# Moving a head's probability scaling one slot later, and its transposes behind the up product

## The reference

```
x  = hidden (8, 512, 512);  xn = layernorm(x)
attention: 16 query heads of 32, ONE key and one value head shared by all,
           rotary positions with a decay, causal mask, softmax over 512 keys,
           projection 512 -> 512 plus bias
shared:    relu(xn @ up.T)**2 @ down.T            (512 -> 1024 -> 512)
routed:    8 of 32 experts a token (2 of 4 groups), 256 -> 256 -> 256 in a latent
out = x + attention(xn) + shared(xn) + routed(xn)
```

## Time and profile before

| what | value |
|---|---|
| median of 3 runs | 1751.81 us (1751.12 to 1755.2) |
| the profiled execution | 1752.61 us, span 1750.6 us |
| PE busy | 1625.1 us, 93% of the span |
| DVE busy | 1201.7 us, 69% |
| ACT busy | 1072.9 us, 61% |
| mean granted clock of TensorE | 0.978 |

### The profile page before, as it was taken

How to read it: one execution, slowest core, us unless ns; L and a number is a source line. 1 busy time by engine, 2 the same in 40 slices (tenths; PEclk the granted TensorE clock), 3 DMA queues, 4 the chain that set the end, 5 groups by cost and what they waited for, 6 DMA issues and landing times.

```text
span 1750.6 us, 40616 instructions
## 1 busy us (share of the span) xinstructions
PE 1625.1 (93%) x10811; PEld 1390.9 (79%) x10811; DVE 1201.7 (69%) x3666; ACT 1072.9 (61%) x2799; POOL 821.5 (47%) x669
## 2 busy tenths in 40 slices
PE   5875779999999999999999999899999999999999
PEld 5765567787777777877777778689999999999987
DVE  6868877877777868777778687355555555555567
ACT  3344455775666757756757577366666666666652
POOL 0212001452444525424434254177777877777760
PEclk9897889999999999999999999999999999999999
DMA  7951722443434434334344344489999999988894
GB/s 280 380 163 43 145 64 84 150 123 119 145 111 149 141 106 143 127 117 152 115 147 137 96 147 134 124 168 192 177 196 189 190 182 203 202 173 158 141 257 184
DMA packets 193090, 273.71 MB, mean 156 GB/s; under 512 B 37400, under 2 KB 133791, under 8 KB 190820
## 3 DMA queue, kind: packets, MB, share of 16 engines
q0 software_dynamic: 60352, 92.59, 24.5%
q1 hardware_dynamic: 77572, 113.01, 22.8%
q10 hardware_dynamic: 54944, 65.52, 12.6%
HBM read 121.83 MB, written 129.67 MB: 144 GB/s over the span
## 4 chain that ended last, share of the span: by engine, by line
PE 63%; DVE 17%; issue 8%; DMA 5%; ACT 4%; POOL 2%; DVEq 1%; SPq 0%; ACTq 0%; POOLq 0%
PE e_psH L1701 12%; PE e_psY L1712 12%; DVE m_sc L1084 5%; PE m_psO L1330 4%; PE m_psU L64 3%; PE m_psT L1308 3%; PE m_psS L1283 3%; PE e_psX L1686 3%; PE m_psU L66 3%; PE m_psU L65 3%; PE m_psY L64 3%; PE m_psY L66 3%; PE m_psY L65 3%; DVE m_sc L1094 3%; ACT m_sc L930 2%
## 5 line engine op out<-in xcount | busy, mean ns | idle before, releaser
L1666 POOL DMA_INDIRECT sums<-e_y,e_where x287 | 446.0, 1554 | 155.0 <-issue 89.3
L852 POOL DMA_INDIRECT slot_rows<-m_row,slots x256 | 266.6, 1041 | 479.9 <-ACT m_sc L930 448.2
L930 ACT ACTIVATE m_sc<-m_sc,m_low 128x512 f32<-128x512 f32 (+3 forms) x512 | 283.8, 556 | 182.1 <-DVE m_low L1084 180.5
L1701 PE MATMUL e_psH<-e_xt,e_w_of 128*128 128x128 f32 x2296 | 303.6, 275 | 3.3 <-ACT e_xt L1561 3.3
L1712 PE MATMUL e_psY<-e_w,e_ht 128*128 x1148 | 295.8, 380 | 2.1 <-ACT e_ht L1572 1.9
L1084 DVE CUSTOM_DVE_ANT_0 m_sc<-m_psS,cst 128x512 f32<-128x512 f32 (+3 forms) x512 | 229.6, 485 | 88.2 <-PE m_psS L1283 85.6
L1701 PEld LDWEIGHTS e_psH<-e_xt,e_w_of 128*128 128x128 f32 x2296 | 279.1, 192 | 3.6 <-ACT e_xt L1561 3.5
L1567 ACT ACTIVATE e_w_of<-e_w 128x512 f32 x287 | 180.9, 630 | 121.4 <-issue 117.1
L1283 PE MATMUL m_psS<-m_ks,m_qs 96*128 96x256 f32 (+2 forms) x512 | 161.4, 375 | 74.1 <-DVE m_low L1084 67.1
L1712 PEld LDWEIGHTS e_psY<-e_w,e_ht 128*128 128x128 f32 x1148 | 196.4, 191 | 17.6 <-issue 3.0
L1622 DVE TENSOR_SCALAR e_where<-e_row,e_shifts 128x1 uint32<-128x1 uint32 x287 | 61.3, 214 | 197.2 <-DMA sums<-e_y,e_where 177.5
(11 more groups left out here) (229 smaller groups left out, 3235.3 us busy)
## 6 DMA issues: line engine op xcount, KB each, us to landing
e_row<-slot_rows ACTq DMA_DIRECT2D x287, 144.5 KB
m_qs<-m_qhi SPq DMA_DIRECT2D x256, 64.0 KB, 2.0
e_w<-in_w SPq DMA_DIRECT2D x256, 64.0 KB
f_xt<-in_x SPq DMA_DIRECT2D x8, 1024.0 KB, 11.0
m_qs<-m_qlo SPq DMA_DIRECT2D x128, 64.0 KB, 2.0
m_res<-in_x SPq DMA_DIRECT2D x8, 1024.0 KB, 6.2
sums<-empty POOLq DMA_DIRECT2D x32, 256.0 KB
partial<-m_res ACTq DMA_DIRECT2D x16, 512.0 KB
```

The source lines that it names most:

```text
L852: pool.indirect_dma_start(out=xs, out_offset=bass.IndirectOffsetOnAxis(ap=slots_sb[:, g, k:k + 1], axis=0), in_=row[g % 2][:, :], in_offse ...
L930: nc.scalar.activation(cols, cols, ACT.Exp, bias=low[:, h % 2, i:i + 1], scale=-1.0, accum_out=total[:, h % 2, i:i + 1]).then_inc(exp_done, 1)
L1666: pool.indirect_dma_start(out=both_sums, out_offset=bass.IndirectOffsetOnAxis(ap=where[u % NY][:, 0:1], axis=0), in_=y[u % NY][:, :], in_o ...
L1701: mm = pe.matmul(psH[u % 2][:, k * P:(k + 1) * P], w1_of[u % 2][:, c * INTER + k * P:c * INTER + (k + 1) * P], xt[u % 2][:, c * P:(c + 1) ...
```

## The change

`scale(s)` on DVE moves from the end of slot s to slot s + 1, between the first and the second pair of masks there; `shared` moves behind the second pair. On PE the first group of transposes moves from ahead of the values and the up product to behind them, so that the three groups stand together but for the queries' product. On ACT relu and square move ahead of the copy of the first group. Nothing is added or left out.

```
@@ act_program
+                    if s < NH:
+                        shared(s)
                     if 0 <= t < NH:
                         ta(t, 0)
-                    if s < NH:
-                        shared(s)
@@ dve_program
                         mask_and_min(s, ROWS[0])
                         mask_and_min(s, ROWS[1])
                     if 1 <= s <= NH:
+                        scale(s - 1)
+                    if s < NH:
+                        mask_and_min(s, ROWS[2])
+                        mask_and_min(s, ROWS[3])
+                    if 1 <= s <= NH:
                         shared(s - 1)
                     if s - 1 in Q_AT:
                         rotate(b, f"q{Q_AT[s - 1]}", (0,))
-                    if s < NH:
-                        mask_and_min(s, ROWS[2])
-                        mask_and_min(s, ROWS[3])
...
-                    if s < NH:
-                        scale(s)
                     if s - 2 in Q_AT:
                         low_part(b, f"q{Q_AT[s - 2]}")
@@ pe_program
                         scores(s, ROWS[2])
                         scores(s, ROWS[3])
-                    if 0 <= t < NH:
-                        transposes(t, 0)
                     if s > HC and s % HC == 1:
                         values(s // HC - 1, (0, 1, 3, 2))
                     if s < NH:
                         up(s)
                     if 0 <= t < NH:
+                        transposes(t, 0)
                         transposes(t, 1)
                     if s in Q_AT:
                         queries(b, Q_AT[s])
                     if 0 <= t < NH:
                         transposes(t, 2)
```

## The result

| | before | after |
|---|---|---|
| median | 1751.69 us (1751.12 to 1755.2, 4 runs) | 1783.39 us (1779.05 to 1784.9, 4 runs) |
| ratio | | 1.0161, 95% interval 1.0139 to 1.0183 |
| profiled execution, span | 1752.61, 1750.6 us | 1782.89, 1780.8 us |
| mean granted clock | 0.978 | 0.974 |

The changed kernel is slower by 1.6%. The prediction said 1778 us, range 1748 to 1798.

A forecast was written before the change was run, and what follows sets the result against it. PE was taken as busiest, above all in attention, waiting 18.3 us for VectorE's masks. Profiled 1752.6 + 23.8 (seven batches at +3.4) - 1.5 (first batch) + 4 (clock) = 1779, so 1778 us; range 1748 to 1798.

The forecast's parts named there:

- The wait before the reciprocal: VectorE idle until ScalarE's last exponential of a head, 76 times, 0.75 us each; the change was to remove it.
- slot 8: Slot with a query product, 8.73 us because VectorE comes late; VectorE would have caught up, so -0.74 us, near 8.0.
- slot 12: Plain slot losing its small wait for masks: 4.77 us becomes 4.57.
- Two small terms: Slot 4, query product after the relu: +0.10 us on 7.89; slot 15, a plain slot, shortened like slot 12.
- Transposes behind up: Slots 5, 9, 13: third transpose group waits for ScalarE's copy of the first; +0.77, +0.77, +0.60 us a batch.
- Rotation behind the squares: Slots 2, 6, 10: VectorE idle 0.7 us during ScalarE's rounding, next mask late; +0.70, +0.80, +0.80 us a batch.
- First batch: Six waits before the reciprocal saved, -5.0 us; transposes waiting for the shared bank, +3.6; taken as -1.5.
- Clock: After every second of seven 2.0 us PE gaps in slot 7, half clock costing 1.2 us: +4, bounds 0 to +27.
- Faster: Freed wait shrinks VectorE's lateness at slots 3, 7, 11; slot 7's first mask before X6+7.06 (slot 6's start); 1741 us; chance 0.14.
- No change: One of the two new waits, transposes' or rounding's, is hidden and the first batch gives 5 us: 1756 us; chance 0.10.
- Much slower: The clock falls after all 21 gaps: 1802 us; chance 0.08.

The follow-up runs named there:

- The first experiment: Changed kernel with the first group of transposes and its copy back ahead of the up product in slots 5, 9, 13 and 17; 1760.95 us, ratio 1.0038.
- e5_transposes_only: Kernel before with only the transposes and the relu moved as in the change, VectorE's order left as it was; 1762.10 us, ratio 1.0046.
- e1_early_group: Changed kernel, first transpose group back before the up product, its copy ahead of the relu, in slots 5, 9, 13, 17; 1760.95 us, ratio 1.0038.
- e2_filled_gap: Changed kernel with eight added matmuls of 512 columns ahead of slot 7's third score, all batches but the first; 1772.55 us, ratio 1.0096.
- e4_result_first: Changed kernel with the addition of the last batch's results ahead of the squares in slots 0 and 1; 1782.46 us, ratio 1.0161.

## Why the prediction was right

The forecast was 5 us below the median. The mechanisms held in the seven later batches; the sizes of the first batch and of the clock were off, in opposite directions, so that the total came out so near is in part luck.

- **The wait before the reciprocal is gone, and that helps little** in the seven batches, as forecast: what PE gained by it is slot 8, which fell to 7.99 us, and slot 12, which fell to 4.57, both as worked out. Two small terms did not come: slot 4 was forecast 0.10 longer from a slot of 7.89 us, where the other six batches have 8.06 to 8.14, and it stayed the same in the mean; slots 15 to 17 together were 0.2 longer in the mean, where slot 15 was to be 0.2 shorter.
- **Transposes behind up.** Forecast 7.85 us for slots 5, 9 and 13; 7.81 measured; slot 13, from 7.26, grew by 0.53 where 0.60 was forecast. The wait was 0.54 us and not the 0.7 named. The first experiment undoes this cost alone, e5_transposes_only makes it alone.
- **Rotation behind the squares.** The wait of 0.70 us, the first mask at 7.86 us after the start of slot 6, and the sums of slots 6 and 7 (11.74 forecast, 11.73 measured without the slow stretch) and of 10 and 11 (11.14, 11.12) came as worked out; slots 2 and 3 took 11.6 us in most batches, 0.8 to 1.1 more than before and 1.0 in the mean, for an estimate of 0.7. A batch was 3.7 us longer in the mean without the slow stretches, for 3.4 forecast: 26 us in seven for 23.8. That PE's down product in slot 2 waits for the addition of results had been missed; it lies under the same lateness.
- **First batch**, the term of -1.5: it measured -10.6, outside the bounds of -5 to +3.6. The step that failed in size is the gain of six waits at 0.84 us, 5.0 in all: 0.84 is a wait of a later batch, and the first batch had twelve, 12.7 us in all. The working did not read its slot 0, where the wait was 3.15 us and a routing instruction of 6.55 us stood behind it. The cost, forecast at 3.6, shows as four waits of 2.9 us in all for the copy. The experiment on the first batch alone confirms the size of the gain. Of the 10.6 us, 4.6 are followed, up to the first mask of slot 1, and some 3 go with the granted clock; how the rest divides over the later slots was not followed up.
- **Clock**, the term of +4: 11 us by the slots, 11 to 12 by filling the gaps; inside the bounds of 0 to 27. Seven stretches came instead of three and a half, and each took 1.6 us instead of 1.2. The rule of the Trainium skill (TensorE: Matmul & The Clock Gate, Why this matters for your kernels) warns only of idle gaps between bursts of matmuls that are longer than these. It is not borne out here: gaps of 2.0 and 1.4 us were followed by the lower clock in some batches, and filling them took it away in all.
- Two errors cancel, then: the first batch gave 9 us more than forecast, the clock took 7 to 8 more, and the seven batches 2 more. What is left, 1.2 us ahead of the first score and 2.6 behind the attention batches, is not explained; no run was made for it. In the ten profiled kernels the first score comes at 113.05 to 115.45 us and the last part takes 658.9 to 662.9, so differences of this size also come between kernels that hardly differ there.
- **Rivals.** *Faster* failed at the place named: the first mask of slot 7 came at 7.86 us, not before 7.06. *No change* failed because neither new wait was hidden. *Much slower* failed on the count of slow stretches, 7 and not 21.

## What to carry to other kernels

A long total of short waits is worth only what the instruction after the wait is holding up; ask for each slot which engine ends last there, and look at the first pass of a loop by itself, where a single wait can stand ahead of a long instruction. When work is moved to another slot, look at what had been covered by it: here the scaling had covered ScalarE's rounding, and the early place of the transposes had covered a copy that frees their bank. Once such covers are restored one by one, the moved step can be worth keeping.

## What was unexpected of the hardware

An idle time of PE of 1.4 or 2.0 us amid matmuls was followed by a granted clock of 0.50 (1.2 GHz) for some 3 us in some batches and not in others, at 1.6 us each. The kernel before, whose longest wait for a mask is 1.2 us, has 1.00 in all four windows of 200 us from 300 to 1100, and so has the kernel with the transposes moved alone, whose longest is 1.4 (once).

The length of a gap alone does not decide, as a count over the seven later batches of four kernels shows:

| kernel | gap of 2.0 us in slot 7 | gap of 1.4 us in slot 11 | gap of 1.4 us in slot 3 |
|---|---|---|---|
| the changed kernel | low clock after 6 of 7 | after 1 of 7 | no such gap |
| e1_early_group | after 1 of 7 | after 4 of 7 | no such gap |
| e2_filled_gap | filled | after 5 of 7 | no such gap |
| e4_result_first | after 2 of 7 | after 1 of 7 | after 5 of 7 |

In the experiment with the early group the 2.0 us gap was spared six times in seven and the 1.4 us gap was not four times, though the edit changes neither. Which property of the work or of its timing decides is left open.
